# Layer 1's offsets: the inverse square root of the variance computed as a power on GpSimd in place of a root on ScalarE and a reciprocal on VectorE

## The reference, cut to what matters

```
x1 = depthwise_conv3x3(x) + dw_b                      # 64 channels, 48x48 pixels, 4 images
mu  = x1.mean(channels)
var = ((x1 - mu) ** 2).mean(channels)
x1  = (x1 - mu) * rsqrt(var + 1e-5) * ln_g + ln_b
x1  = gelu(x1)
offset = x1 @ w_off + b_off                           # 72 columns
mask   = softmax(x1 @ w_mask + b_mask)                # 36 columns
```

## Time and profile before

| what | value |
|---|---|
| median of 3 runs | 1411.65 us (1410.33 to 1412.98) |
| the profiled execution's own time | 1411.69 us |
| its span in the trace | 1409.9 us |
| TensorE matmul, busy | 1119.5 us (79%) |
| VectorE, busy | 986.7 us (70%) |
| GpSimd, busy | 701.7 us (50%) |
| ScalarE, busy | 635.8 us (45%) |
| mean granted TensorE clock | 0.913 |

### The profile page before, as it was taken

One profiled execution on the slowest core, in us unless ns is written; L12 is line 12 of the kernel. 1 busy time (PEld: TensorE's weight loads), 2 busy tenths in 40 slices (PEclk: granted clock), 3 DMA queues, 4 the chain that ended last, 5 costly groups with the idle time before them and its releaser, 6 DMA issues. The chain is left out here.

```text
span 1409.9 us, 32315 instructions
## 1 busy us (share of the span) xinstructions
PE 1119.5 (79%) x13632; PEld 574.1 (41%) x13632; DVE 986.7 (70%) x1209; ACT 635.8 (45%) x1082; POOL 701.7 (50%) x550
## 2 busy tenths in 40 slices
PE   2870059977849999999999767599999999998638
PEld 1440047753315555555555434133333333334313
DVE  3678955666978888888888557846766666676713
ACT  1444024443636666666666526034444444445410
POOL 2001012103347777677777403078888888888500
PEclk9995579998959999999999979889999999999869
DMA  4100000002201011101111004000000000000032
GB/s 84 21 1 0 0 2 3 2 3 48 52 29 30 30 30 37 37 30 30 30 30 44 3 0 135 1 1 2 2 2 2 2 2 1 2 2 2 1 109 68
DMA packets 29012, 31.99 MB, mean 23 GB/s; under 512 B 19212, under 2 KB 21837, under 8 KB 28029
## 3 DMA queue, kind: packets, MB, share of 16 engines
q1 hardware_dynamic: 28861, 29.85, 8.2%
HBM read 21.50 MB, written 5.94 MB: 19 GB/s over the span
## 5 line engine op out<-in xcount | busy, mean ns | idle before, releaser
L2117 POOL TENSOR_TENSOR arena_sb<-arena_sb 128x768 f32<-128x768 f32 x168 | 322.4, 1919 | 121.1 <-ACT arena_sb L2078 100.6
L2078 ACT ACTIVATE arena_sb<-ps 128x768 f32<-128x768 f32 x216 | 174.8, 810 | 242.7 <-PE ps L2007 241.7
L2132 DVE TENSOR_REDUCE arena_sb<-ps 128x4 f32<-128x1536 f32 x108 | 188.2, 1756 | 129.0 <-PE ps L1974 128.8
L1615 DVE TENSOR_TENSOR arena_sb<-ps,arena_sb 120x768 f32<-120x768 f32 x216 | 206.7, 957 | 11.0 <-DVE arena_sb L1610 0.6
L2007 PE MATMUL ps<-arena_sb 33*64 33x384 f32 x1728 | 187.5, 502 | 11.4 <-ACT arena_sb L2078 5.5
L1643 POOL TENSOR_SCALAR xp_sb<-xp_sb 128x384 f32<-128x384 f32 x92 | 137.3, 1492 | 98.0 <-ACT xp_sb L1555 88.7
L1513 PE MATMUL ps<-arena_sb 120*64 120x216 f32 x1536 | 182.2, 359 | 0.0
L2019 PE MATMUL ps<-arena_sb 64*64 64x384 f32 x1728 | 168.1, 488 | 3.4 <-ACT arena_sb L2085 3.4
L1497 PE MATMUL ps<-xn_sb,arena_sb 32*120 32x384 f16 x1728 | 120.8, 353 | 11.3 <-DVE xn_sb L1604 4.3
L1570 ACT ACTIVATE xp_sb<-ps 128x432 f32<-128x432 f32 x192 | 101.8, 530 | 61.0 <-PE ps L1513 60.9
L1610 DVE COPY arena_sb<-ps 120x384 f32<-120x384 f32 x216 | 118.4, 548 | 4.5 <-PE ps L1497 3.3
(11 more groups left out here) (239 smaller groups left out, 1529.5 us busy)
## 6 DMA issues: line engine op xcount, KB each, us to landing
arena_sb<-pixel_major SPq DMA_DIRECT2D x96, 120.0 KB, 2.3
pixel_major<-arena_sb SPq DMA_DIRECT2D x24, 108.0 KB
x_sb<-in_x SPq DMA_DIRECT2D x4, 576.0 KB, 8.4
arena_sb<-arena_sb SPq DMA_DIRECT2D x8, 288.0 KB, 5.6
xn_sb<-in_W SPq DMA_DIRECT2D x1, 2304.0 KB, 8.6
arena_sb<-in_W SPq DMA_DIRECT2D x1, 2304.0 KB, 8.1
out_x<-x_sb SPq DMA_DIRECT2D x24, 96.0 KB, 2.2
filters<-arena_sb SPq DMA_DIRECT2D x4, 144.0 KB, 4.2
```

The costliest lines, as they stand in the source:

```text
L1615: v_.tensor_tensor(bmat[m % 2][:, 2 * CH * t:2 * CH * t + 2 * CH].rearrange("p (e n) -> p e n", e=2), p_y[t % 2], xs[t % 2].rearrange("p ( ...
L2078: act.activation(pt[g % SLOTS].rearrange("p (h n) -> p h n", h=2), p_scores(g), ACT.Exp)\
L2117: pool.tensor_tensor(acc, first, pt[g % SLOTS], ALU.add).then_inc(S["pool_added"], 1)
L2132: v.tensor_reduce(part.rearrange("p (a u j) -> p a u j", a=3, u=NB)[:, a, :, jc], p_m(m), AX.X, ALU.max)\
```

## The change

ScalarE's instruction at L376 no longer takes a square root: with `Identity` it only adds 1e-5 and copies the variance out of PSUM. GpSimd then raises each half to the power -1/2 in place, with the exponent broadcast from one column, and signals VectorE, which goes straight to z.

```diff
@@ ScalarE
-                act.activation(inv, p_var, ACT.Sqrt, bias=k["eps"][:, 0:1]).then_inc(S["root"], 1)
+                act.activation(inv, p_var, ACT.Identity, bias=k["eps"][:, 0:1]).then_inc(S["root"], 1)
@@ VectorE
-                v.wait_ge(S["root"], n + 1)
                 for h in range(2):
-                    v.reciprocal(inv[:, h, :], inv[:, h, :]).then_inc(S["inv"], 1)
                     if n:
                         v.wait_ge(S["gelu"], 2 * n + h - 1)
                     v.wait_ge(S["inv"], 2 * n + h + 1)
@@ GpSimd
+        @block.gpsimd
+        def _(pool):
+            power = k["small"][:, 39:40]
+            pool.memset(power, -0.5).then_inc(S["power"], 1)
+            pool.wait_ge(S["power"], 1)
+            for n in range(PAIRS):
+                pool.wait_ge(S["root"], n + 1)
+                for h in range(2):
+                    pool.tensor_tensor(inv[:, h, :], inv[:, h, :], power.to_broadcast([128, CH]), ALU.pow).then_inc(S["inv"], 1)
```

More of the change, by code:

```diff
@@ L296, in offsets0 @@
     S = {n: signal(k, "off0_" + n) for n in
-         ("bias_ps", "bias", "conv_ps", "sq", "var_ps", "root", "inv", "z", "gelu", "om_ps", "om", "top", "loaded")}
+         ("bias_ps", "bias", "conv_ps", "sq", "var_ps", "root", "inv", "z", "gelu", "om_ps", "om", "top", "loaded", "power")}
     def pair(at):
```

## The result

The changed kernel takes 2119.05 us (median of 4 runs, 2118.68 to 2119.95) against 1411.74 us before: a ratio of 1.50, 95% interval 1.498 to 1.502. That is 707 us more. The forecast was 1506 us, 95 us more, with a range from 1398 to 1630. The sign was right and the size was far off.

A forecast was written before the change was run, and what follows sets the result against it. VectorE's reciprocals were taken to bound the offsets block by a little, TensorE right behind. Twelve powers of 10.4 us less 38.15 gave +86.7 us, TensorE's clock 8, so +94.7 on 1411.69: 1506 us, range 1398 to 1630.

The forecast's parts named there:

- What bounds the kernel, and the loop: Offsets block: a loop of 11.46 us through z, Gelu, Square, variance, root and reciprocals, 1.09 us longer than TensorE's work.
- rival B: The power is cheap, below 2.9 us, and the kernel is faster, 1398 to 1408 us as TensorE becomes the bound; chance 0.15.
- Identity and the table loads: ScalarE in the block: Identity costs the root's 0.90 us; some 10 loads of 1.28 us go, covered by waits, worth nothing.
- The sum 12P - 38.15: Change in us of the block's six loops, P being one power's time: two powers replace the reciprocal stretch; break-even 3.18 us.
- TensorE's clock: Slow tap and variance matmuls after longer gaps in the block: 8 us added, between 3.9 and 12.3.
- First use and hops on GpSimd: Before the first power: code load covered, cost nothing. From root's end to second z: two powers plus 0.25 us of hops.
- How large is P?: One GpSimd power over 128x384: 10.4 us from 20 counted steps; 5.45 us at 10 steps, 20.3 at 40.
- Rival C: The power is dearer than 20 us: at 20.3 us, +217.8 us, so 1630 and beyond; chance 0.16.

The follow-up runs named there:

- identity_for_root: The kernel before with Identity in place of ScalarE's square root alone, VectorE's reciprocals kept: 1412.72 us against 1412.86.
- log_exp: The kernel before with root and reciprocals replaced by logarithm and exponential on ScalarE: 1399.69 us, ratio 0.9893 to 0.9923.
- the first experiment: The kernel before with eight GpSimd powers of several sizes added in the offsets block on scratch columns nothing reads: 1412.18 us against 1412.86.
- one_table_root: The kernel before with one ScalarE function, Abs_reciprocal_sqrt, in place of root and reciprocals: 1397.62 us, ratio 0.9867 to 0.9904.

## Why the prediction was wrong

- *What bounds the kernel, and the loop.* Right but for one leg. The loop of the change is variance, Identity, two powers, z, and back to the variance by the slow taps in four loops, by Gelu and Square in one. The sum left the taps out of the loop and had their slowness in the term for the clock, so the total does not suffer. TensorE's own work was a little too high (10.37 for 10.09 us), which touches rival B alone.
- *Identity and the table loads.* Right, shown by identity_for_root: about ten loads fewer, no change in time. The Trainium skill's 2.66 us a switch (ScalarE: Activation LUTs, "What ACT_TABLE_LOAD costs") is not what these traces show: in log_exp a load of 1.28 us starts at 66.91, when the logarithm before it ends (65.99 + 0.90), and the next instruction starts at 68.21.
- *The sum 12P - 38.15.* Right. With the measured P it gives 12 x 61.52 - 38.15 = +700.1 us; the block grew by 708.1. With the clock's few us on top it held at P = 3.05, 10.5 and 61.5.
- *TensorE's clock.* Right in kind and size: 708.1 - 700.1 leaves 8.0 us, and I had taken 8 between bounds of 3.9 and 12.3. Three more groups of slow taps (2.84 for 1.54) and variances of 2.2 to 2.9 for 1.56 to 1.60 in five loops are what it is made of. That it came out at the very number is luck.
- *First use and hops on GpSimd.* Right at nothing; 2P + 0.14 was measured for 2P + 0.25.
- *How large is P?* This is the step that failed: "My estimate is 10 steps at the very least, 20 as the likely count, 40 with the special cases and a careful logarithm", at 0.495 us for each. The power takes 61.52 us. By the same row it would be (61.52 - 0.50) / 0.495 = 123 steps, three times my highest count and six times my likely one. The price of a step was taken from stock instructions, where each operation over 384 columns costs 0.495 us; that row says nothing on how the function is written. What it is made of, the runs do not show; they show that it is 0.159 us a column with no dependence on base, exponent or partitions. The same error made the range wrong: I wrote that no row bounds P from above, and then let 40 counted steps bound the range.
- *Rival B* went the other way. Its price for a cheap instruction was near right (13.7 us for 15.7 in the block). The Trainium skill's rule that spoke for it (GPSIMD Engine Reference, section 3.1) is some 3 operations a cycle; by it the 0.159 us a column, 191 cycles at the prediction's 1.2 GHz, would be some 570 operations, an estimate. The count of 20 steps with it gave 2.2 us, and the instruction takes 61.5. The runs do not tell whether the rule or the count fails.
- *Rival C* ("dearer than 20 us") is what happened, with a chance of 0.16, but its point of 20.3 us was still three times too low.

## What to carry to other kernels

Price an instruction that no row shows by measuring it alone before building on it: a few sizes beside idle time on its engine, as in the first experiment, cost the kernel nothing and would have given the answer to 1%. A sum of the path with the unknown price left as a letter is worth the work even so: here its break-even (3.2 us) was right, and it says at once what any replacement may cost. And a reciprocal behind a root on the path can be taken out where the root already is, with one ScalarE function, if its exactness is enough: 1.2% here, where the table loads stood beside a wait and cost nothing.

## What the runs showed of the hardware

- A power on GpSimd in float32 costs 0.3 to 0.4 us and 0.159 us for each column, on 1 partition as on 128: 61.52 us for 128x384, 74 times the multiply of the same shape (0.826 us) and 24 times VectorE's reciprocal (2.54 us).
- 61 us of powers on GpSimd beside a busy VectorE slowed neither the block nor the kernel (1412.18 us against 1412.86).
- ScalarE's logarithm and exponential each had a table load ahead of them, 1.28 us, every time; one over the root is one function with one load (one_table_root).
- After gaps of 15, 57 and 120 us TensorE's first 16 taps took the same 2.84 us for 1.54. The variance behind them took 1.8 to 2.0 us after 15 us (2.3 after one of 18), 2.2 after 57, 2.2 to 2.7 after 120, for 1.56: it varies as much at one length of gap as between lengths. After a gap of 2.67 us the taps took 2.84 us in the kernel before and 1.54 in identity_for_root.
